# A recurrence of 256 steps: one fp32 product moves from VectorE to GpSimd, and the output is added step by step

## The reference, cut to what matters

```python
def step(carry, xs):
    h, c = carry
    xi_t, xf_t, xg_t, xo_t = xs
    i_t = jax.nn.sigmoid(xi_t + h @ V_i)
    g_t = jnp.tanh(xg_t + h @ V_c)
    o_t = jax.nn.sigmoid(xo_t + h @ V_o)
    c_new = h * c + i_t * g_t
    h_new = o_t * jnp.tanh(c_new)
    return ((h_new, c_new), h_new)
...
t = t + _L2_ffn_ref(_ln_t(t), ...)
```

## Time and profile before

| what | value |
|---|---|
| time, median of 3 runs | 1316.96 us (1315.24 to 1318.18) |
| profiled execution, first to last instruction (span) | 1314.1 us |
| recurrence, from its first step's matmuls to its last step | 426.5 us of the span |
| busy in the span: PE, DVE, ACT, POOL | 77%, 64%, 39%, 21% |

### The profile page before, as it was taken

One profiled execution on the slowest core, in us unless ns is written; L12 is line 12 of the kernel. 1 busy time (PEld: TensorE's weight loads), 2 busy tenths in 40 slices (PEclk: granted clock), 3 DMA queues, 4 the chain that ended last, 5 costly groups with the idle time before them and its releaser, 6 DMA issues. The chain is left out here.

```text
span 1314.1 us, 27039 instructions
## 1 busy us (share of the span) xinstructions
PE 1012.1 (77%) x9646; PEld 581.0 (44%) x9646; DVE 846.2 (64%) x2450; ACT 514.9 (39%) x1332; POOL 274.8 (21%) x376
## 2 busy tenths in 40 slices
PE   6877868677998566666666666667973999999996
PEld 2366643343677354544445454543531333333332
DVE  7697638644656655555555555554356888888885
ACT  3544524352544223222322232223542545545442
POOL 4504112100000000000000000000100455556556
PEclk9889988777999855555555555557985999999998
DMA  7000002000000000000000000000002755555550
GB/s 234 1 1 1 1 2 81 0 1 0 1 0 1 1 1 0 0 0 0 0 0 0 0 0 0 0 0 1 0 1 70 157 119 136 114 128 133 113 133 9
DMA packets 10675, 47.39 MB, mean 36 GB/s; under 512 B 1520, under 2 KB 5744, under 8 KB 6128
## 3 DMA queue, kind: packets, MB, share of 16 engines
q1 hardware_dynamic: 10608, 46.49, 14.5%
HBM read 43.86 MB, written 2.62 MB: 35 GB/s over the span
## 5 line engine op out<-in xcount | busy, mean ns | idle before, releaser
L1638 PE MATMUL wide<-ls_h,ls_v 128*128 128x16 f16 x2304 | 104.6, 176 | 145.4 <-DVE ls_h L1737 142.0
L2147 ACT ACTIVATE ex_gated<-wide,unscale 128x1024 f32<-128x1024 f32 x128 | 142.3, 1114 | 140.2 <-PE wide L2113 139.6
L2163 DVE TENSOR_TENSOR ex_hid<-wide,ex_gated 128x1024 f32<-128x1024 f32 x128 | 155.9, 1223 | 40.0 <-ACT ex_gated L2147 28.0
L1638 PEld LDWEIGHTS wide<-ls_h,ls_v 128*128 128x128 bf16 x2304 | 81.5, 105 | 214.4 <-DVE ls_h L1737 214.3
L2089 POOL TENSOR_TENSOR ex_acc<-ex_part,ex_acc 128x512 f32<-128x512 f32 x120 | 152.5, 1271 | 95.0 <-DVE ex_part L2179 80.8
L1727 DVE TENSOR_TENSOR_SCAN ls_cells<-ls_terms 128x48 f32<-128x48 f32 x256 | 73.9, 289 | 124.1 <-ACT ls_terms L1662 124.1
L1662 ACT ACTIVATE ls_terms<-wide 128x32 f32<-128x32 f32 x256 | 54.4, 213 | 229.1 <-PE wide L1643 229.1
L2125 PE MATMUL wide<-ex_hid,w 128*64 128x512 f32 x512 | 116.7, 598 | 0.0
L2113 PE MATMUL wide<-xh,wh 64*128 64x512 f16 x512 | 99.2, 384 | 5.5 <-PEq L81 3.7
L2113 PE MATMUL wide<-xh,wl 64*128 64x512 f16 x512 | 98.3, 380 | 0.0
L2113 PE MATMUL wide<-xl,wh 64*128 64x512 f16 x512 | 98.3, 380 | 0.0
(11 more groups left out here) (368 smaller groups left out, 1863.9 us busy)
## 6 DMA issues: line engine op xcount, KB each, us to landing
ex_d<-route SPq DMA_DIRECT2D x64, 512.0 KB, 6.3
par_attn<-in_attn SPq DMA_DIRECT2D x1, 2704.0 KB, 13.2
par_rest<-in_rest SPq DMA_DIRECT2D x1, 2523.5 KB, 18.6
L_xin<-in_x SPq DMA_DIRECT2D x8, 256.0 KB, 5.7
w<-in_w SPq DMA_DIRECT2D x1, 2048.0 KB, 8.1
out<-ex_acc SPq DMA_DIRECT2D x16, 128.0 KB, 3.5
w<-in_w SPq DMA_DIRECT2D x1, 512.0 KB, 9.1
route<-ro_dt SPq DMA_DIRECT2D x2, 256.0 KB, 2.0
```

The lines of the kernel that those rows point to most:

```text
L1638: pe.matmul(ig[:, g, :] if g < 2 else o, vp[part][:, g, :], h1[:], start=False, stop=False, skip_group_check=True)
L2147: act.activation(gated[:, n % 2, :], pair_of_up(n // GS, 2 * (n % GS))[:], ACT.Silu, scale=m.unscale[:, 0:1]).then_inc(s["gated_ready"], 1)
L2163: dve.tensor_tensor(hid[:, n % (2 * GS), :], pair_of_up(n // GS, 2 * (n % GS) + 1)[:], gated[:, n % 2, :], ALU.mult).then_inc(s["hid_ready ...
```

## The change

The fp32 product moves from DVE to POOL, into one tile h32 that is written anew in each step. POOL waits in each step for og, for the end of the last step's addition to the stream (semaphore out_ready), and for tc, in this order. DVE keeps the fp16 product; before it takes h2 it waits for its own h1 and for POOL's h32. The ring hs, the tiles hx and unscale, POOL's two instructions per eight steps and the semaphore "scaled" go. Instead DVE adds each step's output to its column of the stream itself, behind hc.

```diff
-        hs = sb("hs", [P, 2 * STEPS, HB])
-        hx, unscale = sb("hx", [P, 2, STEPS, HB]), sb("unscale", [P, STEPS, HB])
+        h32 = sb("h32", [P, HB])
...
         @block.gpsimd
         def _(pool):
-            pool.sem_inc(s["scaled"], 2)
-
-            pool.memset(unscale[:], 1.0 / SC).then_inc(s["split_step"], 1)
-            pool.wait_ge(s["split_step"], 1)
             with pool.Fori(0, HW // (2 * STEPS)) as i:
                 for b in range(2):
-                    j = 2 * i + b
-                    pool.wait_ge(s["h32_ready"], STEPS * (j + 1))
-                    pool.tensor_tensor(hx[:, b], hs[:, STEPS * b:STEPS * (b + 1), :], unscale[:], ALU.mult)\
-                        .then_inc(s["scaled"], 1)
-                    pool.wait_ge(s["scaled"], j + 3)
-                    x = xa_bt[:, :, bass.ds(STEPS * j, STEPS)]
-                    pool.tensor_tensor(x, hx[:, b].rearrange("p s b -> p b s"), x, ALU.add).then_inc(s["out_ready"], 1)
+                    for q in range(STEPS):
+                        t = 2 * STEPS * i + STEPS * b + q
+                        pool.wait_ge(s["og_ready"], t + 1)
+                        pool.wait_ge(s["out_ready"], t + 1)
+                        pool.wait_ge(s["tc_ready"], t + 1)
+                        pool.tensor_tensor(h32[:], og[:], tc[:], ALU.mult).then_inc(s["h32_ready"], 1)
...
+            dve.sem_inc(s["out_ready"], 1)
             dve.wait_ge(m.moe_landed, 32)
             with dve.Fori(0, HW // (2 * STEPS)) as i:
                 for b in range(2):
-                    dve.wait_ge(s["scaled"], 2 * i + b + 1)
                     for q in range(STEPS):
...
                         dve.wait_ge(s["tc_ready"], t + 1)
                         dve.wait_ge(s["og_ready"], t + 1)
-                        h32 = hs[:, STEPS * b + q, :]
                         dve.tensor_tensor(h1[:], og[:], tc[:], ALU.mult).then_inc(s["h1_ready"], 1)
-                        dve.tensor_tensor(h32, og[:], tc[:], ALU.mult).then_inc(s["h32_ready"], 1)
+                        dve.wait_ge(s["h1_ready"], t + 2)
                         dve.wait_ge(s["h32_ready"], t + 1)
-                        dve.tensor_tensor(h2[:], h32, h1[:], ALU.subtract).then_inc(s["h2_ready"], 1)
-                        dve.scalar_tensor_tensor(hc, h32, 1.0 / SC, cell, ALU.mult, ALU.mult)\
+                        dve.tensor_tensor(h2[:], h32[:], h1[:], ALU.subtract).then_inc(s["h2_ready"], 1)
+                        dve.scalar_tensor_tensor(hc, h32[:], 1.0 / SC, cell, ALU.mult, ALU.mult)\
                            .then_inc(s["hc_ready"], 1)
+                        x = xa_bt[:, :, bass.ds(t, 1)].rearrange("p b t -> p (b t)")
+                        dve.scalar_tensor_tensor(x, h32[:], 1.0 / SC, x, ALU.mult, ALU.add)\
+                           .then_inc(s["out_ready"], 1)
```

More of the change, by code:

```diff
@@ L1589, in lstm_stage @@
                  "gates_ready cell_ready tc_ready og_ready h1_ready h32_ready h2_ready hc_ready "
-                 "scaled out_ready scale_step turned spread scale_ready").split()
+                 "out_ready scale_step turned spread scale_ready").split()
         top, ones, wscale = sb("top", [P, 4]), sb("ones", [1, P]), m.wscale
```

## The result

| what | before | after |
|---|---|---|
| time, median of 4 runs each | 1316.70 us (1315.24 to 1318.18) | 1354.04 us (1351.56 to 1355.61) |
| span of the profiled execution | 1314.1 us | 1351.7 us |
| first h1 to last h1 of the recurrence | 424.1 us | 460.7 us |

The change costs 37.3 us: ratio 1.0285, 95% interval 1.0265 to 1.0304. The forecast was 1350 us, slower. Of the 37.6 us that the span grew, 36.6 lie between the first and the last h1 of the recurrence. Of the runs that follow, one execution is left out: the fourth of the first experiment, which took 3258 us where its other three took 1328 to 1330. Lines shift: after the change POOL's product is L1678, the scan L1721, h1 L1730, h2 L1733, hc L1734, the addition to the stream L1737, ACT's gates L1661 and tc L1667, PE's two groups L1637 and L1642.

The account below looks back on a forecast made before the run. The prediction took the recurrence to be bound by latency, with h2 on the path. A later h2 (+41.0 us) less the scans' lengthening (7.7) gave +33.3 on 1316.96, 1350 us; range 1328 to 1362.

Parts of the forecast that it names:

- The bound: Recurrence: a closed chain of latencies, 1.63 us a step, with h2 on the path and no engine full.
- What it removes: Scan on DVE: without POOL's two batched instructions its lengthening goes, 30 ns x 256 = 7.7 us, all on the path.
- Part 1: POOL's start: tc's wait, written last, has its own entry, 0.15 us after tc; start at +0.12 from h1's start.
- the second early wait: POOL's wait for out_ready, long over: its entry may stand behind tc's, nothing to 0.02 us, taken as 0.01.
- Part 2: POOL's 128x16 product: 221 ns, bounds 206 and 243, ending at +0.35 from h1's start.
- Part 3: DVE's wait for h32, written second, has its own entry: 0.10 us after POOL's end, h2 at +0.45.
- Part 4: After h2, 0.16 us late: PE, ACT and the scan follow one to one, 256 x 0.16 = +41.0 us.
- DVE's addition at nothing: Addition to the stream behind hc: 0.09 to 0.18 us a step, covered by DVE's idle time before the scan.
- Carried after all: Late waits on POOL and DVE ride on their instructions: h2 0.01 us late, -5 us, 1312 us; chance 10%.
- Only one is carried: DVE's wait for h32 rides on h2 through a register operation between its waits: +15 us, 1332 us; chance 10%.
- The two engines block each other: POOL's product must wait for DVE's h1: about 0.05 us a step, 12.8 us more, 1363 us; chance 7%.
- the third rival: POOL's product held by DVE's h1, as the skill's shared-port lock says: 12.8 us more, 1363 us; chance 7%.

Follow-up runs that it names:

- the first experiment: The changed kernel with POOL's wait for tc written before those for og and out_ready; 1328.38 us, ratio 1.0096 to the kernel before the change.
- the third experiment: The changed kernel with POOL's wait for tc and DVE's wait for h32 each written first; 1308.99 us, ratio 0.9941 to before.
- The fourth experiment: The changed kernel without POOL in the recurrence: DVE takes both products and adds each step's output to the stream; 1308.22 us, ratio 0.9942 to before.
- the fifth experiment: The changed kernel with the wait for out_ready moved from POOL to DVE, before og; 1344.43 us, ratio 1.0218 to before.
- the second experiment: The changed kernel with DVE's wait for h32 written before that for h1, and the output gate's wait comparing with t + 2; 1333.67 us, ratio 1.0126 to before.
- The eighth experiment: The third experiment with the two waits before h1 swapped, og before tc, so h1 starts after POOL's product; 1334.27 us, ratio 1.0138 to before.
- seventh: The kernel before the change plus POOL's fp32 product each step, written into the ring; POOL's two batched instructions stay; 1360.63 us, ratio 1.0345 to before.
- sixth: The changed kernel with DVE's loop written out for 32 steps in 8 passes, other engines unchanged; 1370.38 us in a single run.
- ninth: The changed kernel with one more wait on DVE, for out_ready before og, POOL keeping its three waits; 1351.59 us, ratio 1.0269 to before.

## Why the prediction was right

**The bound.** "Whatever delays h2 by x delays the step by x" holds in the regular steps of every kernel here: h2 later by 0.165 us in the change, step longer by 0.167 (medians); in the third experiment h2 at +0.30, step back at 1.63. One link of the chain was read a little off: ACT's gates start 0.02 us before the end of PE's second group (655.74 + 0.33 against 656.05), not behind it. Nothing hangs on that.

**What it removes.** The scans' lengthening was 7.7 us. The fourth experiment, which has only this part, gained 8.5; in the trace of the change the scan's maximum is 258 ns. The wait for "scaled", at nothing, is inside that.

**Part 1, when POOL starts.** That the wait written first is carried and the others stand in front is shown by the first experiment, which changes nothing but the order. Predicted was +0.13 after h1 (0.12, and 0.01 for the second early wait); it is 0.135 (mean; 600.27 - 600.13 = 0.14 in the step shown). The term that was mis-sized is the second early wait: I took 0.01 us for it, from nothing to 0.02, and the fifth experiment measured 0.026, since it makes the late entry longer, from 17 to 43 ns. 16 ns x 256 = 4 us; the 0.15 us of the earlier trace rows was itself 8 ns too long (142 without it), which gave 2 us back. That the two errors half cancel is luck.

**Part 2, POOL's product.** 221 ns between its neighbours by the earlier trace rows, 221 measured. With 206 and 243 as the bounds, a hit to the nanosecond is partly luck too.

**Part 3, when DVE hears.** 0.10 us by the earlier trace rows, 0.103 measured (median); 0.033 carried, by the second experiment, where the earlier trace rows had given 0.03.

**Part 4 and the sum.** 0.16 x 256 = 41.0 predicted; 0.167 x 256 = 42.8 measured, by the length of the regular step. Against it stand 7.7 removed, and 1.7 us for the longer steps where a pass ends, which the prediction did not have: it said that there would be none. 42.8 - 7.7 + 1.7 = 36.8, close to the 36.6 between the first and the last h1. The 0.7 us that are left to the 37.3 of the medians are within what the runs scatter.

**DVE's addition at nothing.** The cover held: 0.43 us idle before the scan after it, and 180 ns for one, where the bounds were 0.09 to 0.18.

**The rivals.** *Carried after all* is the third experiment: 1309 where 1312 was given, so the price was right and the condition was not met. *Only one is carried*: the register operation for t + 2 is there (L1731, 40 ns), but it stands in front of both waits. In the step shown it runs from 600.15 to 600.19, before h1 ends at 600.30, so it takes neither of them, and the wait for h32 has its own entry. With POOL carried and DVE not, the first experiment took 1328; the other way, which is this rival, the second took 1334, where 1332 was given. *The two engines block each other* did not come about: POOL's product starts while h1 still has 0.04 us to run in the change and 0.13 in the third experiment, and takes 221 and 220 ns. The eighth experiment shows what the blocking is worth when the order is turned.

The Trainium skill ("SBUF — State Buffer", section "SBUF: two separate sides") says of such a pair that the later one waits for the whole instruction of the first. The traces agree that the later one is held, in both orders, but not for quite so long. DVE behind POOL is in the seventh and eighth runs (460 instead of 176 ns, 224 instead of 176). POOL behind a longer instruction of DVE is in the kernel before, outside the recurrence. L196, an addition of POOL, starts there behind DVE's L312 and, in another place, behind L319, which takes one of its two inputs from PE's output and not from SBUF (timeline of the kernel before):

```profile
33.37 0.78 DVE L312 SCALAR_TENSOR_TENSOR L_acc<-xpad,L_taps,L_acc 128x528 f32<-128x528 f32 x1
33.55 1.76 POOL L196 TENSOR_TENSOR xa<-L_branch,xa 128x512 f32<-128x512 f32 x1
...
227.24 0.68 DVE L319 TENSOR_TENSOR xa<-wide,L_acc 128x512 f32<-128x512 f32 x1
227.50 1.28 POOL L196 TENSOR_TENSOR xa<-L_branch,xa 128x512 f32<-128x512 f32 x1 [6.11 <-ACT L_branch L272]
```

With 0.60 us of L312 left, L196 takes 1.76 us; behind L319 it takes 1.28, and 1.26 to 1.29 with DVE idle. In the held pairs, and for hc and the scan in the earlier trace rows, the later instruction is longer by what was left of the first when it started, less 0.11 to 0.15 us. That settles the third rival: h1 never has more than 0.13 us left when POOL starts, too little to hold POOL's product, while that product's 0.22 us are enough to hold h1.

## What to carry to other kernels

Where several waits stand in front of an instruction in a chain bound by latency, write the one that comes last in time first: here it was worth 91 ns on POOL and 70 ns on DVE a step, 45 us in all (some 2 of them from the longer steps, which went too), and turned a loss of 37 us into a gain of 8. Before work is moved to an idle engine, look for what the move itself can save: with the product on DVE h2 came 0.295 us after h1, with it on POOL at best 0.299, since the handover and back ate what DVE was spared. Batches of an idle engine beside the chain are not free: here they held the scan in every eighth step, and adding each step's output on DVE, in its idle time, was the faster way.

## What the runs showed that I had not expected

- A POOL entry that holds two waits takes 43 ns and one with a single wait 17, and the instruction behind it starts later by the difference, though one of the two waits is long over.
- An instruction of DVE that starts 0.02 us behind one of POOL is held until POOL's is over, and POOL's is held behind DVE's as well, if enough of DVE's is left (0.48 us with 0.60 left, nothing with 0.13). Which of the two starts first in the recurrence was decided by the order of two waits.
- At one place in DVE's code, 16 steps from the loop's start, h2 came 0.10 us late in each pass, and 0.35 in the first, behind a wait entry that was itself on time: at the end of the second pass the entry is over at 519.25 and h2 starts at 519.41, where a regular step has 0.045 us between them. In a body of 32 steps the place kept its 0.35 in each pass, the end of a pass stalled DVE by about 2.5 us, and the body was loaded again in each pass. That it is a matter of the code's place is shown by the sixth and ninth runs; what the 0.10 us is made of in passes that load nothing stays open.
